# Transposing the attention weights of differential attention by DMA alone, with a third pair of score banks

## The chip, the cores and the metric

One Trainium2 chip, eight cores, each running the same program on its own batch element of a batch of eight. The time is the device time of the slowest core, in microseconds (us).

## The reference, cut to what matters

Per batch element: 2048 tokens, width 2048, 16 query heads and 4 key/value heads of size 128. Each head has two query and two key projections, and its attention weights are a second softmax over the difference of two softmaxes.

```python
xn = _layernorm(x)
q = _rope((xn @ Wq).reshape(b, s, 16, 256));  k = _rope((xn @ Wk).reshape(b, s, 4, 256))
energy = einsum('bqhad,bkhad->bahqk', qd, kd)          # a = 0, 1: two score maps
energy = where(causal, -1e30, energy)
scores = softmax(energy / sqrt(128), axis=-1)
diff = softmax(where(causal, -1e30, scores[:, 0] - lam * scores[:, 1]), axis=-1)
att  = einsum('bhqv,bvhd->bqhd', diff, v)
att  = att * rsqrt(mean(att * att, -1) + 1e-8) * rms_w * (1 - LAM_INIT)
s = att.reshape(b, s, E) @ Wo
g = silu(ffn(xn))      # Hadamard transform, 8-bit activations, ternary weights, squared relu, twice
return x + s * g
```

## The kernel before

The program is a row of stages, one after the other. The stage that matters here is the attention, from about 2795 to 6785 us of the profiled span. Before it lie the weight scales, the layer norm and the projections, after it the output projection and the two layers of the feed-forward part.

The attention loops over 16 heads, and in each head over four groups of queries (`qc` = 0 to 3, 512 queries each). A group has four query tiles of 128 rows (`qs` = 0 to 3; `qt` = 4 qc + qs is the tile's number in the sequence). For each query tile, in program order:

- **Scores.** For each chunk of up to 512 keys (`nch` = qc + 1 of them, the last one is the diagonal chunk), TensorE makes the two score maps into the PSUM banks `psE0[b]` and `psE1[b]` (L746, L750). VectorE adds the causal triangle to the last 128 columns of the diagonal chunk (`trif`, L762, L764). ScalarE takes the exponentials and their sums (L769, L772), which frees the bank pair. There are two pairs, used in turn.
- **Difference.** VectorE works out the two reciprocals (`rstep`, L781 to L786) and the difference (`dif`, L798 to L806), and ScalarE its exponential into `Pf` (`expP`, L811).
- **Normalize.** VectorE scales the row into the bfloat16 tile `Pb` (`pnorm`, L822 to L825).
- **Transpose.** The tile's weights, qt + 1 blocks of 128x128, are brought into `PT`, keys on partitions. Blocks of even number go by a DMA transpose each, issued by SyncE (`ptp_e`, L837). Blocks of odd number are transposed one by one on TensorE into one of two PSUM buffers `psT4` (L849), and copied to `PT` by VectorE (L862) or ScalarE (L867) in turn.

After the four tiles of a group: `zset` (L880) sets the six 128x128 blocks of `PT` that lie above the diagonal to zero on VectorE; `attmm` (L890) multiplies values by `PT`, 4 qc + 4 matmuls; then come the square (L900), its sum over partitions (L903), a copy (L907), a small store by SyncE (L910) and the scaled copy of the result (L915).

What orders the work is written out by hand. Each step names the engine and the earlier steps it waits for, and the class `Ch` turns this into semaphore waits. Every engine works through its own steps in program order, so a step that waits holds all later steps of that engine. SyncE, besides, waits after a step for the landing of its own transfer when a later step names it as the last of its lane; for `ptp_e` this holds for the fourth tile of a group alone. The step `zset` waits for "the step added just before it" (`after=[steps.__len__() - 1] + ...`), whatever step that is. `pnorm` and the transposes of a group wait for the `attmm` of the group before. The next head's queries are loaded by SyncE ahead of the head's first tile.

Of the kernel before, what the change touches and what calls it, by code (L numbers as in the profile page):

```python
# [8 lines left out]
F32 = mybir.dt.float32  # L9
BF16 = mybir.dt.bfloat16  # L10
# [4 lines left out]
T = 2048  # L15
# [140 lines left out]
def build_program(taps=(), upto=99):  # L156
    nc = bass.Bass("TRN2", target_bir_lowering=False)
# [28 lines left out]
    out = dt("out", [T, E], F32, "ExternalOutput")  # L186
# [13 lines left out]
    with st:  # L200
# [23 lines left out]
        idn_s = sbuf("idn_s", [128, 128], BF16)  # L224
# [6 lines left out]
        with ExitStack() as ph:  # L231
# [13 lines left out]
                          lambda e, inc, _l=loads: [inc(e.dma_start(out=d[:, :], in_=s[:, :]), 16)  # L245
                                                    for d, s in _l])]
# [22 lines left out]
        with ExitStack() as ph:  # L269
# [12 lines left out]
            for i, (w, r, c) in enumerate(tiles):  # L282
# [4 lines left out]
                                  lambda e, inc, _w=w, _r=r, _c=c, _i=i:  # L287
# [3 lines left out]
                                  after=[prev_red] if prev_red >= 0 else -1))  # L291
# [178 lines left out]
        with ExitStack() as ph:  # L470
# [24 lines left out]
            def add(stp):  # L495
                steps.append(stp)
                return len(steps) - 1
# [133 lines left out]
        with ExitStack() as ph:  # L631
# [25 lines left out]
            taub = sb("taub", [128, 512], F32)  # L657
            taurow = sb("taurow", [1, 2 * 512], F32)
            psE0 = [ph.enter_context(nc.psum_tensor(f"psE0{i}", [128, 512], F32)) for i in range(2)]
            psE1 = [ph4i.enter_context(nc.psum_tensor(f"psE1{i}", [128, 512], F32)) for i in range(2)]  # L660
            psAt = ph4i.enter_context(nc.psum_tensor("psAt", [128, 512], F32))
            psRo = ph4i.enter_context(nc.psum_tensor("psRo", [128, 512], F32))
            psT4 = [ph4i.enter_context(nc.psum_tensor(f"psT4{i}", [128, 128], BF16))
                    for i in range(2)]
            psRp = psRo

            qc_glob = [0]
# [1 line left out]
            tptb_ctr = [0]  # L669
            tp_evac_b = {0: -1, 1: -1}  # L670
            steps = []
            idx_exp_bank = {0: -1, 1: -1}
            idx_attmm_prev = -1
            idx_attts_prev = -1
            idx_sq_prev = -1
# [21 lines left out]
            for g in range(KVH):  # L697
                gp_ = g % 2
                for hl in range(4):
# [27 lines left out]
                    for qc in range(4):  # L727
# [5 lines left out]
                        for qs in range(4):  # L733
# [4 lines left out]
                            for kc in range(nch):  # L738
                                cw = 512 if kc < qt // 4 else (qt % 4 + 1) * 128
                                isdiag = (kc == qt // 4)  # L740
                                bank = pair_glob[0] % 2
                                pair_glob[0] += 1

                                def mme(e, inc, _qt=qt, _kc=kc, _cw=cw, _b=bank,
                                        _gp=gp_, _hp=hp_):
                                    e.matmul(psE0[_b][:, 0:_cw],  # L746
                                             qh[_hp][:, _qt * 128:(_qt + 1) * 128],
                                             kg[_gp][:, _kc * 512:_kc * 512 + _cw],
                                             start=True, stop=True)
                                    inc(e.matmul(psE1[_b][:, 0:_cw],  # L750
                                                 qh[_hp][:, T + _qt * 128: T + (_qt + 1) * 128],
                                                 kg[_gp][:, T + _kc * 512: T + _kc * 512 + _cw],
                                                 start=True, stop=True))
                                i_mm = add(Step("tensor", 1, mme,
                                                after=[i_qload, i_kvload,
                                                       idx_exp_bank[bank]]), tag="E")
                                kv_used[gp_].append(i_mm)
                                q_used[hp_].append(i_mm)
                                i_pre = i_mm
                                if isdiag:  # L760
                                    def trif(e, inc, _cw=cw, _b=bank):
                                        e.tensor_add(psE0[_b][:, _cw - 128:_cw],  # L762
                                                     psE0[_b][:, _cw - 128:_cw], tri_s[:, :])
                                        inc(e.tensor_add(psE1[_b][:, _cw - 128:_cw],  # L764
                                                         psE1[_b][:, _cw - 128:_cw], tri_s[:, :]))
                                    i_pre = add(Step("vector", 1, trif, after=[i_mm]), tag="E")

                                def expf(e, inc, _kc=kc, _cw=cw, _b=bank, _p=par):
                                    e.activation(e0b[:, _p * T + _kc * 512: _p * T + _kc * 512 + _cw],  # L769
                                                 psE0[_b][:, 0:_cw], AF.Exp, scale=ISQ,  # L770
                                                 accum_out=A0[:, _p * 4 + _kc:_p * 4 + _kc + 1])
                                    inc(e.activation(e1b[:, _p * T + _kc * 512: _p * T + _kc * 512 + _cw],  # L772
                                                     psE1[_b][:, 0:_cw], AF.Exp, scale=ISQ,
                                                     accum_out=A1[:, _p * 4 + _kc:_p * 4 + _kc + 1]))
                                i_exp = add(Step("scalar", 1, expf,
                                                             after=[i_pre, last_pn[par]]), tag="E")
                                idx_exp_bank[bank] = i_exp
                                idx_exp_last = i_exp
# [50 lines left out]
                                            after=[idx_expP_last, idx_attmm_prev]), tag="P")  # L829
                            last_pn[par] = i_pn  # L830

                            n_even = (qt + 2) // 2
                            n_odd = (qt + 1) // 2

                            def ptp_e(e, inc, _qt=qt, _qs=qs, _of=PTof):
                                for kt in range(0, _qt + 1, 2):
                                    inc(e.dma_start_transpose(  # L837
                                        PT[:, _of + kt * 512 + _qs * 128: _of + kt * 512 + (_qs + 1) * 128],
                                        Pb[:, _qs * T + kt * 128: _qs * T + (kt + 1) * 128]), 16)
# [1 line left out]
                                            after=[i_pn] + idx_ptp_prev[ptpar]), tag="T")  # L841
                            idx_ptp_cur.append(i_tp)
                            last_tp[par] = i_tp
                            for kt in range(1, qt + 1, 2):
                                tb = tptb_ctr[0] % 2
                                tptb_ctr[0] += 1
                                i_tt = add(Step("tensor", 1,
                                               lambda e, inc, _kt=kt, _qs=qs, _tb=tb:
                                               inc(e.transpose(psT4[_tb][:, :],  # L849
                                                               Pb[:, _qs * T + _kt * 128:  # L850
                                                                  _qs * T + (_kt + 1) * 128],
                                                               idn_s[:, :])),
                                               after=[i_pn, tp_evac_b[tb]] + idx_ptp_prev[ptpar]),
                                           tag="T")
                                ee = "scalar" if (tptb_ctr[0] % 2 == 0) else "vector"

                                def tevac(e, inc, _kt=kt, _qs=qs, _of=PTof, _tb=tb):
                                    inc(e.tensor_copy(
                                        PT[:, _of + _kt * 512 + _qs * 128:
                                           _of + _kt * 512 + (_qs + 1) * 128],  # L860
                                        psT4[_tb][:, :]) if False else
                                        e.tensor_copy(  # L862
                                        PT[:, _of + _kt * 512 + _qs * 128:
                                           _of + _kt * 512 + (_qs + 1) * 128],
                                        psT4[_tb][:, :]))
                                def tevac_s(e, inc, _kt=kt, _qs=qs, _of=PTof, _tb=tb):
                                    inc(e.copy(out=PT[:, _of + _kt * 512 + _qs * 128:  # L867
                                                      _of + _kt * 512 + (_qs + 1) * 128],
                                               in_=psT4[_tb][:, :]))
                                i_ev4 = add(Step(ee, 1, tevac_s if ee == "scalar" else tevac,  # L870
                                                 after=[i_tt]), tag="T")
                                tp_evac_b[tb] = i_ev4
                                idx_ptp_cur.append(i_ev4)
                        zblocks = [(kt, qs) for kt in range(4 * qc + 4) for qs in range(4)
                                   if 4 * qc + qs < kt]

# [526 lines left out]
```

How the kernel before makes its waits and increments, by code:

```python
                def body(eng, _e=ename):  # L125
                    for i, s in enumerate(steps):
                        if s.eng != _e:
                            continue
                        preds = _preds(i, s)
                        if preds:
                            tg = {}
                            for j in preds:
                                ln, c = post[j]
                                tg[ln] = max(tg.get(ln, 0), c)
                            for ln, c in tg.items():
                                eng.wait_ge(self.sems[ln], c)
                        else:
                            for ln, c in base.items():
                                if c > 0:
                                    eng.wait_ge(self.sems[ln], c)
                        mysem = self.sems[s._lane]
                        got = {"n": 0}
                        def inc(instr, k=1, _g=got, _s=mysem):
                            _g["n"] += k
                            return instr.then_inc(_s, k)
                        s.fn(eng, inc)
                        assert got["n"] == s.inc, \
                            f"step {i} ({s.eng}): declared inc {s.inc} != emitted {got['n']}"
                        if s.eng in ("sync", "gpsimd") and i in waited:
                            eng.wait_ge(mysem, post[i][1])
# [54 lines left out]
        def vsync(e, instr):  # L206
            instr.then_inc(vssem, 1)
            vs_n[0] += 1
            e.wait_ge(vssem, vs_n[0])
            return instr
```

## Time and profile before

| | us |
|---|---|
| median of 2 runs | 10589.99 |
| lowest and highest | 10569.17, 10610.82 |
| profiled execution | 10586.41 |
| its span on the slowest core (core 6) | 10584.8 |
| spans of the eight cores | 10537.4 to 10584.8 |

The profile is that of one execution on core 6. Its engines are PE (TensorE matmul), PEld (TensorE weight load), DVE (VectorE), ACT (ScalarE), POOL (GpSimd) and SP (SyncE). SPq stands for SyncE's sequencer, which issues DMAs and is not counted as a busy engine. The rows read from the trace stand in a section of their own below.

### The profile page before, as it was taken

The numbers are of one execution on the slowest core, as the hardware profiler recorded it, in microseconds if no ns is written. First come the engines' busy times: TensorE is split into PE (matmuls) and PEld (weight loads), VectorE is DVE, ScalarE is ACT, GpSimd is POOL, SyncE is SP. The second block draws the span as 40 slices with busy tenths as digits, with TensorE's granted clock in tenths as the row PEclk, the third lists the DMA queues.
The fourth block names the chain that finished last, engine by engine and source line by source line (L and its number), as shares of the span: only waits on it lengthen the run. The fifth ranks groups of instructions, "written<-read, shape, count | busy, mean of one in ns | idle before, by whom it ended". The sixth has DMA issues, their size and how long they took to land. (4 is left out here: it accounts for less than half of the span.)

```text
span 10584.8 us, 65816 instructions; the slowest of 8 cores (10537.4 to 10584.8 us)
## 1 busy us (share of the span) xinstructions
PE 3650.6 (34%) x12334; PEld 1337.9 (13%) x12334; DVE 3547.4 (34%) x9994; ACT 2182.6 (21%) x6008; POOL 961.7 (9%) x1684
## 2 busy tenths in 40 slices
PE   0010004555522222222222222355577201014777
PEld 0000002222200000000000000012233100001222
DVE  5114432222333333333333333210011465653221
ACT  0220002222333333333333333200122100000110
POOL 0000004444000000000000000013111000000111
PEclk9999999777655555555555555557788655556777
DMA  6210004333100000000000000012333101011222
GB/s 235 71 49 19 18 24 92 67 67 70 37 14 14 13 19 14 14 14 20 15 16 20 14 14 14 8 14 34 92 103 100 40 17 32 17 32 56 78 85 70
DMA packets 622508, 462.31 MB, mean 44 GB/s; under 512 B 366329, under 2 KB 572394, under 8 KB 611362
## 3 DMA queue, kind: packets, MB, share of 16 engines
q1 hardware_dynamic: 437538, 269.24, 9.2%
q0 software_dynamic: 184576, 188.85, 7.9%
q8 instruction: 120, 1.97, 0.1%
q14 instruction: 274, 2.24, 0.1%
HBM read 350.52 MB, written 98.57 MB: 42 GB/s over the span
## 5 line engine op out<-in xcount | busy, mean ns | idle before, releaser
L849 PE MATMUL psT<-idn_s,Pb 128*128 128x128 bf16 x1024 | 268.0, 265 | 2206.0 <-DVE Pb L825 2076.2
L1298 PE MATMUL psD<-K,tsl 128*128 128x512 bf16 x2048 | 613.9, 473 | 86.5 <-DVE tsl L1276 86.5
L1057 PE MATMUL psU<-xqs,tsl 128*128 128x512 bf16 x2048 | 522.8, 423 | 180.4 <-DVE tsl L1047 180.4
L980 POOL DMA_DIRECT2D wost<-wo x256 | 136.0, 592 | 4296.3 <-DVEq L123 4258.1
L811 ACT ACTIVATE Pf<-e0b 128x512 f32<-128x512 bf16 (+3 forms) x640 | 362.1, 566 | 781.0 <-DVE e0b L802 515.9
L602 PE MATMUL psP<-xns,wqst 128*128 128x512 bf16 x2048 | 487.1, 402 | 28.7 <-ACT Xs L612 26.2
L769 ACT ACTIVATE e0b<-psE 128x512 bf16<-128x512 f32 (+3 forms) x640 | 341.6, 534 | 422.4 <-DVE psE L764 264.5
L746 PE MATMUL psE<-kg,qh 128*128 128x512 bf16 (+3 forms) x640 | 327.9, 513 | 270.3 <-DMA qh<-qT_h 151.0
L849 PEld LDWEIGHTS psT<-idn_s,Pb 128*128 128x128 bf16 x1024 | 106.9, 104 | 2464.2 <-issue 2451.9
L616 DVE TENSOR_TENSOR m1b<-Xc,ctab 128x512 f32<-128x512 f32 x160 | 110.7, 692 | 858.0 <-ACT Xs L612 857.9
L890 PE MATMUL psAt<-PT,vg 128*128 128x512 bf16 x640 | 254.1, 574 | 370.3 <-DMA PT<-Pb 370.3
L762 DVE TENSOR_TENSOR psE<-psE,tri_s 128x128 f32<-128x128 f32 x256 | 76.6, 299 | 830.4 <-PE psE L750 830.4
L750 PE MATMUL psE<-kg,qh 128*128 128x512 bf16 (+3 forms) x640 | 343.6, 539 | 0.0
L990 PE MATMUL psE<-attT,wost 128*128 128x512 bf16 x1024 | 260.0, 421 | 234.1 <-DMA wost<-wo 234.1
L772 ACT ACTIVATE e1b<-psE 128x512 bf16<-128x512 f32 (+3 forms) x640 | 339.3, 530 | 0.0
L1102 DVE TENSOR_TENSOR W2f<-W2f 128x256 f32<-128x256 f32 x640 | 218.3, 419 | 335.8 <-ACT W2f L1161 332.5
L602 PE MATMUL psP<-xns,wkst 128*128 128x512 bf16 x512 | 126.8, 411 | 508.0 <-DMA wqst<-wq 507.4
L1298 PEld LDWEIGHTS psD<-K,tsl 128*128 128x128 bf16 x2048 | 233.9, 116 | 442.3 <-issue 306.9
L867 ACT COPY PT<-psT 128x128 bf16<-128x128 bf16 x512 | 136.2, 266 | 729.9 <-PE psT L849 729.9
L1191 PE MATMUL psR<-mrow,onr 1*128 1x256 f32 x16 | 9.5, 694 | 789.0 <-DVE betar L1186 789.0
L1057 PEld LDWEIGHTS psU<-xqs,tsl 128*128 128x128 bf16 x2048 | 216.2, 107 | 486.9 <-issue 297.2
L526 POOL DMA_DIRECT2D wqst<-wq x512 | 273.0, 975 | 13.0 <-issue 13.0
(180 smaller groups left out, 6670.3 us busy)
## 6 DMA issues: line engine op xcount, KB each, us to landing
xns<-xnT_h SPq DMA_DIRECT2D x256, 128.0 KB
wstg<-wupT SPq DMA_DIRECT2D x512, 64.0 KB
h_h<-h2b POOLq DMA_DIRECT2D x128, 256.0 KB, 2.5
W2f<-h_h SPq DMA_DIRECT2D x256, 128.0 KB
wst<-wdnT SPq DMA_DIRECT2D x512, 64.0 KB
PT<-Pb SPq DMA_TRANSPOSE x1152
wst<-wupT SPq DMA_DIRECT2D x16, 1024.0 KB
wst<-wupT POOLq DMA_DIRECT2D x16, 1024.0 KB, 5.5
```

Of the source, the lines that this page charges most:

```text
L526: inc(e.dma_start(out=wqst[_p][:, (hl * 2 + c2) * 2048 + ec * 128: (hl * 2 + c2) * 2048 + (ec + 1) * 128], in_=wq[ec * 128:(ec + 1) * 128, ...
L602: mm = e.matmul(psP[_b][:, :], _w[:, _wc + ec * 128: _wc + (ec + 1) * 128], xns[_xp][:, ec * 512:(ec + 1) * 512], start=(ec == 0), stop=(e ...
L746: e.matmul(psE0[_b][:, 0:_cw], qh[_hp][:, _qt * 128:(_qt + 1) * 128], kg[_gp][:, _kc * 512:_kc * 512 + _cw], start=True, stop=True)
L750: inc(e.matmul(psE1[_b][:, 0:_cw], qh[_hp][:, T + _qt * 128: T + (_qt + 1) * 128], kg[_gp][:, T + _kc * 512: T + _kc * 512 + _cw], start=T ...
L769: e.activation(e0b[:, _p * T + _kc * 512: _p * T + _kc * 512 + _cw], psE0[_b][:, 0:_cw], AF.Exp, scale=ISQ, accum_out=A0[:, _p * 4 + _kc:_ ...
L772: inc(e.activation(e1b[:, _p * T + _kc * 512: _p * T + _kc * 512 + _cw], psE1[_b][:, 0:_cw], AF.Exp, scale=ISQ, accum_out=A1[:, _p * 4 + _ ...
L811: inc(e.activation(Pf[:, _kc * 512: _kc * 512 + _cw], e0b[:, _p * T + _kc * 512: _p * T + _kc * 512 + _cw], AF.Exp, accum_out=Zc[:, _p * 4 ...
L849: inc(e.transpose(psT4[_tb][:, :], Pb[:, _qs * T + _kt * 128: _qs * T + (_kt + 1) * 128], idn_s[:, :])),
L890: mm = e.matmul(psAt[:, :], vg[_gp][:, kt * 128:(kt + 1) * 128], PT[:, _of + kt * 512: _of + (kt + 1) * 512], start=(kt == 0), stop=(kt == ...
L990: mm = e.matmul(psS[_b][:, :], wost[_p][:, ec * 128:(ec + 1) * 128], attT[:, ec * T + _tc * 512: ec * T + (_tc + 1) * 512], start=(ec == 0 ...
L1057: mm = e.matmul(psU[_b][:, :], tsl[_p][:, ec * 128:(ec + 1) * 128], xqs[:, ec * T + _tc * 512: ec * T + (_tc + 1) * 512], start=(ec == 0), ...
L1298: mm = e.matmul(psD[_b][:, :], tsl2[_p][:, ec * 128:(ec + 1) * 128], K2[:, ec * T + _tc * 512: ec * T + (_tc + 1) * 512], start=(ec == 0), ...
```

## The change

Three edits, all in the attention stage.

1. All blocks of a query tile go by DMA transpose: `ptp_e` loops over every block instead of every second one, and the loop over the odd blocks (the transposes on TensorE and their copies on VectorE and ScalarE) is gone. Over a head, SyncE issues 136 DMA transposes instead of 72, and 64 TensorE transposes with 64 copies go.
2. The two PSUM buffers `psT4` are gone, and a third pair of score banks `psE0[2]`, `psE1[2]` takes their place. Chunks use the three pairs in turn.
3. Nothing is edited in `zset`, but the step added just before it is now another one: `ptp_e` of the group's fourth tile, where it was the last copy out of `psT4`.

```diff
-            psE1 = [ph4i.enter_context(nc.psum_tensor(f"psE1{i}", [128, 512], F32)) for i in range(2)]
+            psE0.append(ph4i.enter_context(nc.psum_tensor("psE02", [128, 512], F32)))
+            psE1 = [ph4i.enter_context(nc.psum_tensor(f"psE1{i}", [128, 512], F32)) for i in range(3)]
...
-            psT4 = [ph4i.enter_context(nc.psum_tensor(f"psT4{i}", [128, 128], BF16))
-                    for i in range(2)]
...
-            idx_exp_bank = {0: -1, 1: -1}
+            idx_exp_bank = {0: -1, 1: -1, 2: -1}
...
-                                bank = pair_glob[0] % 2
+                                bank = pair_glob[0] % 3
...
-                            n_even = (qt + 2) // 2
-                            n_odd = (qt + 1) // 2
+                            n_even = qt + 1
+                            n_odd = 0
 
                             def ptp_e(e, inc, _qt=qt, _qs=qs, _of=PTof):
-                                for kt in range(0, _qt + 1, 2):
+                                for kt in range(0, _qt + 1, 1):
                                     inc(e.dma_start_transpose(
...
-                            for kt in range(1, qt + 1, 2):
-                                tb = tptb_ctr[0] % 2
-                                tptb_ctr[0] += 1
-                                i_tt = add(Step("tensor", 1,
...
-                                               inc(e.transpose(psT4[_tb][:, :],
...
-                                               after=[i_pn, tp_evac_b[tb]] + idx_ptp_prev[ptpar]),
-                                           tag="T")
-                                ee = "scalar" if (tptb_ctr[0] % 2 == 0) else "vector"
...
-                                i_ev4 = add(Step(ee, 1, tevac_s if ee == "scalar" else tevac,
-                                                 after=[i_tt]), tag="T")
-                                tp_evac_b[tb] = i_ev4
-                                idx_ptp_cur.append(i_ev4)
```

## Rows read from the trace of the kernel before

**Rows 1.** The page: the span in 40 slices, in tenths.

```profile
PE   0010004555522222222222222355577201014777
...
PEclk9999999777655555555555555557788655556777
```

**Rows 2.** Waits in the attention: who waited for whom, total us, times, longest.

```profile
PE psT L849 <- DVE Pb L825: 2076.2, 240, 11.3
...
PE psAt L890 <- DMA PT<-Pb: 370.3, 64, 9.1
...
DVE PT L880 <- ACT PT L867: 43.8, 64, 1.2
```

**Rows 3.** Waits of SP's own queue in the attention, same columns.

```profile
SPq L136 <- DVE Pb L825: 1761.6, 256, 10.2
```

**Rows 4.** Timeline of SP, first group, then last head: start, us, what, how many.

```profile
2801.67 22.70 SPq L837 DMA_TRANSPOSE PT<-Pb  x6
...
6549.32 23.21 SPq L837 DMA_TRANSPOSE PT<-Pb  x6
...
6587.30 35.94 SPq L837 DMA_TRANSPOSE PT<-Pb  x14
...
6640.30 50.10 SPq L837 DMA_TRANSPOSE PT<-Pb  x22
...
6711.52 62.79 SPq L837 DMA_TRANSPOSE PT<-Pb  x30
```

**Rows 5.** Timeline of SP, single stretches: bursts of 4 and 8, two slow issues.

```profile
6618.31 4.92 SPq L837 DMA_TRANSPOSE PT<-Pb  x4
...
6764.28 10.02 SPq L837 DMA_TRANSPOSE PT<-Pb  x8
...
2839.81 1.81 SPq L837 DMA_TRANSPOSE PT<-Pb  x1
...
6730.53 2.28 SPq L837 DMA_TRANSPOSE PT<-Pb  x1
```

**Rows 6.** Line 837: duration in ns, minimum, median, maximum, first and last start.

```profile
L837 SPq DMA_TRANSPOSE PT<-Pb x1152: 1094/1232/2555, 2801.7 to 6773.1; - x192
```

**Rows 7.** Timeline, last head, tiles 0 to 2: start, us, engine, line, operation.

```profile
6548.89 0.29 DVE L825 TENSOR_SCALAR Pb<-Pf,r 128x128 bf16<-128x128 f32 x1
6549.09 0.29 DVE L762 TENSOR_TENSOR psE<-psE,tri_s 128x128 f32<-128x128 f32 x1
...
6554.10 0.35 DVE L825 TENSOR_SCALAR Pb<-Pf,r 128x256 bf16<-128x256 f32 x1
...
6555.85 0.30 DVE L762 TENSOR_TENSOR psE<-psE,tri_s 128x128 f32<-128x128 f32 x1 [0.54 <-PE psE L750]
```

**Rows 8.** Timeline, last head, tile 4 to tile 5.

```profile
6586.61 0.55 DVE L825 TENSOR_SCALAR Pb<-Pf,r 128x640 bf16<-128x640 f32 x1
...
6589.18 0.60 ACT L769 ACTIVATE e0b<-psE 128x512 bf16<-128x512 f32 x1 [0.80 <-PE psE L750]
...
6590.33 0.38 ACT L769 ACTIVATE e0b<-psE 128x256 bf16<-128x256 f32 x1
...
6595.89 0.62 DVE L825 TENSOR_SCALAR Pb<-Pf,r 128x768 bf16<-128x768 f32 x1
```

**Rows 9.** Timeline, last head, end of the group of tiles 4 to 7.

```profile
6617.44 0.75 DVE L825 TENSOR_SCALAR Pb<-Pf,r 128x1024 bf16<-128x1024 f32 x1
6618.44 0.60 PE L849 MATMUL psT<-idn_s,Pb 128*128 128x128 bf16 x2 [8.17 <-DVE Pb L825]
...
6620.51 0.87 DVE L880 MEMSET PT<- 128x128 bf16 x6 [0.62 <-ACT PT L867]
6624.68 3.57 PE L890 MATMUL psAt<-PT,vg 128*128 128x512 bf16 x8 [4.76 <-DMA PT<-Pb]
```

**Rows 10.** Timeline of PE: the values' matmuls of the last two groups.

```profile
6691.89 5.09 PE L890 MATMUL psAt<-PT,vg 128*128 128x512 bf16 x12 [6.42 <-DMA PT<-Pb]
...
6775.75 5.00 PE L890 MATMUL psAt<-PT,vg 128*128 128x512 bf16 x16 [7.79 <-DMA PT<-Pb]
```

More of the change, by code:

```diff
@@ L843, in build_program @@
                             last_tp[par] = i_tp
-                            for kt in range(1, qt + 1, 2):
-                                tb = tptb_ctr[0] % 2
-                                tptb_ctr[0] += 1
-                                i_tt = add(Step("tensor", 1,
-                                               lambda e, inc, _kt=kt, _qs=qs, _tb=tb:
-                                               inc(e.transpose(psT4[_tb][:, :],
-                                                               Pb[:, _qs * T + _kt * 128:
-                                                                  _qs * T + (_kt + 1) * 128],
-                                                               idn_s[:, :])),
-                                               after=[i_pn, tp_evac_b[tb]] + idx_ptp_prev[ptpar]),
-                                           tag="T")
-                                ee = "scalar" if (tptb_ctr[0] % 2 == 0) else "vector"
[L857 to L869, printed above, removed]
-                                i_ev4 = add(Step(ee, 1, tevac_s if ee == "scalar" else tevac,
-                                                 after=[i_tt]), tag="T")
-                                tp_evac_b[tb] = i_ev4
-                                idx_ptp_cur.append(i_ev4)
                         zblocks = [(kt, qs) for kt in range(4 * qc + 4) for qs in range(4)
```

## The prediction, made before the changed kernel was timed

> **What bounds the kernel now.** The slices of the page [rows 1] come first. In the attention, slices 11 to 25, PE stands at 2 and 3 tenths and no engine is full. The stage is therefore a chain of waits and not a full engine, and its length is what it takes to go through that chain. The list of waits for this stretch shows the two links that the change touches [rows 2]. PE waits 2076.2 us for `pnorm` with a transpose at the head of its queue, 240 times: every score matmul of the next query tile stands behind these transposes. And 64 times, once in a group, PE waits for the landing of the DMA transposes before it can multiply by the values: 370.3 us. The third view is SP's own queue [rows 3]: it idles 1761.6 us for `pnorm`. That is SP's whole slack ahead of its transposes.
>
> The timeline of SP gives the length of each group [rows 4]: from the first issue of tile 0 to the end of the last issue of tile 3 it takes 23.21, 35.94, 50.10 and 62.79 us in the last head. Over all 64 such stretches (64 rows, the first 22.70, the last 62.79) the means are 23.2, 36.1, 50.7 and 63.2, together 173.3 us a head. What follows in a group (landing, the values' matmuls, square, sum, copy, the first tile of the next group) hardly depends on who transposed. So I compare this stretch before and after.
>
> **What one DMA transpose costs.** SP is held for the whole issue: the median record of line 837 lasts 1232 ns [rows 6]. A burst of four takes 4.92 us, one of eight 10.02 [rows 5], so each further one costs (10.02 - 4.92) / 4 = 1.275 us. Besides, 42 of the 1152 records, one in 27, last over 1.3 us; the first and last of them are 1.81 and 2.28 [rows 5], about 0.8 over the median, which adds 0.03 each. I take 1.305 us. The engines behind keep up: the values' matmuls start 6624.68 - (6618.31 + 4.92) = 1.45 us after the last issue of a burst of four, and 6775.75 - (6764.28 + 10.02) = 1.45 after one of eight [rows 5, 9, 10]. If transfers piled up, the longer burst would land later. So the price is the issue on SP, and it adds up.
>
> The Trainium skill ("VectorE: DVE Perf Modes", The three transpose paths) gives 390 ns for a 128x128 bf16 transpose on TensorE and 1309 ns by the DMA crossbar, and its rules say to use TensorE where PSUM will do. That rule speaks against this change, and the trace agrees with its DMA figure within 3%; with 1.309 in place of my 1.305 the sum would move by less than 10 us.
>
> **What the removal gives.** Without transposes in PE's queue, the scores of the next tile are done long before they are wanted, and ScalarE goes on to the first chunks while VectorE normalizes. Before, this happens only from tile 0 to tile 1, since tile 0 has no odd block: the triangle of tile 1 starts 0.20 us after the start of tile 0's scaling [rows 7]. From tile 1 to tile 2 it starts 6555.85 - 6554.10 = 1.75 after it; with the row above as the pattern (0.20, and 0.06 for the longer scaling) it would be 0.26. That saves 1.5 us. Tile 3 saves about 1.8, since its score matmuls and the scaling before it are wider (an estimate). In group 1 the exponentials of tile 5's diagonal chunk start at 6590.33 [rows 8]. After the change the first chunk's exponentials, 6590.33 - 6589.18 = 1.15 us, need not wait for the scaling that starts at 6586.61 (ScalarE is free by then), so they are over by 6587.7. The triangle follows the scaling by the same pattern: 0.46 after 6586.61, two additions of some 0.5 together and 0.1 of handover, 6587.7 as well. That saves 2.6 to 2.7 us, and about as much or a little more for tile 6. These times are the chain's. The question is whether SP keeps up.
>
> **Group by group,** first issue to end of last issue, after the change:
> - Group 0, 10 transposes: the chain rules. The 23.2 shrink by 1.5 + 1.8, and the last burst grows from two transposes to four, 2 x 1.275: 23.2 - 3.3 + 2.5 = 22.4.
> - Group 1, 26 transposes: tile 5's scaling starts 6595.89 - 6586.61 = 9.3 us after tile 4's [rows 8], 9.35 with the longer scaling, and after the change 6.65 (five transposes take 6.5, so SP just waits). From there the chain would take some 7.2 us to tile 6 (an estimate: 6.65 and about 0.5 for 128 more keys), but six transposes take 7.8: SP rules. 6.65 + 21 x 1.305 = 34.0.
> - Group 2, 42 transposes: SP is never free. 42 x 1.305 = 54.8.
> - Group 3, 58 transposes: 58 x 1.305 = 75.7.
>
> Together 187.0 (unrounded) against 173.3 us: **+13.7 us a head**. Groups 0 and 1 gain about 0.8 and 2.1, group 2 loses 4.1, group 3 loses 12.5. What the shorter chain gives in groups 2 and 3 is hidden behind SP.
>
> **The step nobody edited.** `zset` waits for the step before it. That was the last copy out of `psT4`: 43.8 us over 64 groups, and the six memsets were over 3.3 us ahead of the values' matmuls (6620.51 + 0.87 against 6624.68) [rows 2, 9]. Now that step is the fourth tile's `ptp_e`, so the memsets start when the transposes have landed, and the matmuls wait for them: 0.87 for the six [rows 9], and a handover from VectorE to PE, which takes 6618.44 - (6617.44 + 0.75) = 0.25 [rows 9]. 1.1 us x 4 groups = **+4.4 us a head**. At least it costs the 0.87 alone (3.5 a head).
>
> **At nothing** I cost three things. The 64 copies a head that leave VectorE and ScalarE are already in the savings above, or lie beside SP's longer burst. The third bank pair: with one chunk the next tile needs one pair, and with three or four the exponentials free a pair every 1.15 us, so that a second pair came back in time as well; its cover is the wait for SP, and were that gone it would be part of the faster rival below. The larger number of landings: 1.45 us after the last issue, as now. Unknown is the clock of the values' matmuls, which come after a longer idle time of PE. In the last head 12 of them take 5.09 us, 0.42 each, which is the 1.2 GHz level, and 16 take 5.00 [rows 10], partly at 2.4 GHz. Were all sixteen at the lower level it would be 6.8: at most +1.8 a head, +29 us, at least nothing. I take nothing into the sum and keep the 29 for the range.
>
> **The sum.** (13.7 + 4.4) x 16 heads = +290 us on the profiled execution's 10586.4, which is 3.6 under the median of the runs: 10876 us, taken as 10875, 2.7% slower. 2% of 10590 is 212 us, about what a measurement of this kernel can tell from no change.
>
> **The rivals.**
> - *Same mechanism, cheaper issues: within 2%.* By the groups above the loss a head is 121 x (price) - 139.9 us (121 transposes are in the terms where SP rules). The 2% line (13.2 a head) lies at 1.265 us each, and a burst of eight costs 10.02 / 8 = 1.25 [rows 5] when counted from a fresh start. With 1.25 it is 11.4 a head, +182 us, and with the memsets at 0.87 as well 10.5, +168: 10755. For it: the slow issues could fall where SP waits anyway. Against it: they come once in 27 transposes, busy or not, and three of four groups now have no wait left.
> - *Issues in a long burst run at the price of a lone one.* The shortest record is 1.094 [rows 6], 1.10 with the step to the next. Then groups 2 and 3 take 46.2 and 63.8, groups 0 and 1 about 21.9 and 30.5: 162.4 + 4.4 against 173.3, -6.5 a head, -104 us: 10480. Against it: the second to eighth of a burst never run so fast now.
> - *The transposes are as good as free: faster.* If SP only hands them over and the chain rules everywhere, each tile but a group's first saves what its diagonal exponentials gain: 3.3 a head in group 0, about 9.4 in group 1, and by the same reckoning some 16 in group 2 and 20 in group 3. 49 x 16 = 780 us, less 70 for the memsets: about 9875. It decides as soon as a transpose costs less than some 1.03 us of SP (6.7 more a head than in the rival above, over some 104 transposes). Against it stand the bursts of four and eight.
> - *Longer bursts meet a limit the bursts of eight don't show* (SP held by a full queue). Then each issue costs more; 10% on 1.305 gives 15.8 more a head, +253: 11130. Against it: no growth of the landing time from four to eight.
>
> For the free-transposes rival the Trainium skill has a rule too ("Advanced Engine Details and Errata", X-Bar Transpose): such a DMA is as fast as a regular one. The trace has SP held 1.232 us by each, whatever the transfer itself takes, so I give that reading little.
>
> **How the numbers follow.** My case, SP as the bound at 1.28 to 1.34 us with the memsets on the path: 0.66. Cheaper issues, within 2%: 0.22. Price of a lone issue: 0.04, also within 2%. Free transposes: 0.04. A queue limit: 0.04. So faster 0.04, within 2% 0.26, slower 0.70. The predicted time is 10875. The range runs from 10755 (1.25 each, memsets alone) to 10965 (1.33 each for +48, clock +29, and some slack); the last three cases lie outside.
>
> **What would show it.** SP's bursts in groups 2 and 3 should be one unbroken row, 42 and 58 transposes in about 55 and 76 us; the wait of SP for `pnorm` should fall from 1761.6 us to some 600, the first tile of each group and group 0. PE's wait of 2076.2 should vanish and reappear as a wait before the values' matmuls, over 1000 us in place of 370.3, released by the memsets of `zset` (or the landing). Group 0 and 1 should be slightly shorter than before. I am wrong if SP still waits for `pnorm` in group 3, if the spacing of issues isn't about 1.28, or if `attmm` starts ahead of the memsets.

## The result, and the profile after

| | before | after |
|---|---|---|
| median of the runs, us | 10630.1 (10 runs) | 10800.2 (11 runs) |
| profiled execution | 10586.4 | 10797.1 |
| its span, slowest core | 10584.8 (core 6) | 10795.5 (core 0) |

The ratio after to before is 1.0178, 95% interval [1.0151, 1.0204]: 1.8% slower. (The ratio is close to that of the runs' means, 10811.7 and 10623.1; the two medians alone would give 1.0160.) The median is inside the forecast range and 75 us under the predicted 10875.

First the page of the changed kernel, slices of the span in tenths, as in [rows 1].

```profile
PE   0010006555321111111111111155477311113776
...
PEclk9999998777655555555555555557688655556777
```

PE is emptier in the attention, 1 tenth instead of 2 and 3, and the stage is no shorter. Its granted clock still stands at 5 tenths, the 1.2 GHz level. Now the waits in the attention (who waited for whom, us in total, times, longest), first those of the engines, then those of SP's queue, which answer [rows 2, 3].

```profile
PE psAt L859 <- DVE PT L849: 2498.7, 64, 56.6
...
DVE PT L849 <- DMA PT<-Pb: 1463.7, 64, 44.3
```

```profile
SPq L136 <- DVE Pb L824: 634.7, 128, 10.4
```

PE's wait for `pnorm` (2076.2 us) is gone. In its place PE waits 2498.7 us before the values' matmuls, and what releases it is the memsets of `zset`. These in turn wait 1463.7 us for the landing of the transposes; before they waited 43.8 us for a copy. SP's own wait for `pnorm` fell from 1761.6 to 634.7 us: its slack is used up. The timeline of SP for the last head (start, us, what, how many) shows where, against the last four rows of [rows 4].

```profile
6749.90 22.64 SPq L836 DMA_TRANSPOSE PT<-Pb  x10
...
6787.67 33.35 SPq L836 DMA_TRANSPOSE PT<-Pb  x26
...
6840.31 54.12 SPq L836 DMA_TRANSPOSE PT<-Pb  x42
...
6916.27 73.84 SPq L836 DMA_TRANSPOSE PT<-Pb  x58
7000.58 0.51 SPq L879 DMA_DIRECT2D msb<-msrow  x1
```

The first two groups are shorter than before (23.21 and 35.94), the last two longer (50.10 and 62.79). The 58 transposes of group 3 take 73.84 / 58 = 1.273 us each without a pause. Over 16 heads the stretches' means are 22.6, 33.4, 53.6 and 74.2, together 183.7 us against 173.3.

Last, the end of the last group, which answers [rows 9, 10].

```profile
6988.88 1.23 SPq L836 DMA_TRANSPOSE PT<-Pb  x1
6991.44 0.87 DVE L849 MEMSET PT<- 128x128 bf16 x6 [42.39 <-DMA PT<-Pb]
6992.56 5.36 PE L859 MATMUL psAt<-PT,vg 128*128 128x512 bf16 x16 [54.78 <-DVE PT L849]
```

From the end of the last issue (6990.11) to the matmuls it is 2.45 us, where it was 1.45. Six memsets of 0.87 and a handover of 0.25 lie between.

**Where the 211 us of the two spans come from.** SP's store at the end of the attention is the row 7000.58 above; in the kernel before it is this one.

```profile
6783.40 0.51 SPq L910 DMA_DIRECT2D msb<-msrow  x1
```

From the first transpose to this store the attention took 6783.40 - 2801.67 = 3981.7 us before [rows 4]. After it took 7000.58 - 2794.74 = 4205.8 (2794.74 is the start of its first transpose): +224 us. Of these (183.7 - 173.3) x 16 = 166 lie in SP's stretches and 1.0 x 64 = 64 between last issue and matmuls; the rest (-6) is in the matmuls and first tiles. The stages around the attention, which have no edit, were 13 us faster in this execution than in that of the kernel before.

### The profile page after: what moved, and what is told of

The parts are those of the page before. It is cut to its first block and busy times, and to the rows that moved or that the text cites. A ratio compares the mean times of both kernels' runs of the same rounds, so it can differ in the third digit from the quotient of the medians.

```text
span 10795.5 us, 60187 instructions; the slowest of 8 cores (10727.6 to 10795.5 us)
## 1 busy us (share of the span) xinstructions
PE 3336.1 (31%) x11310; PEld 1216.9 (11%) x11310; DVE 3420.3 (32%) x9482; ACT 2015.3 (19%) x5496; POOL 962.0 (9%) x1684
## 3 DMA queue, kind: packets, MB, share of 16 engines
q1 hardware_dynamic: 601378, 302.93, 10.6%
## 5 line engine op out<-in xcount | busy, mean ns | idle before, releaser
L859 PE MATMUL psAt<-PT,vg 128*128 128x512 bf16 x640 | 250.2, 567 | 2498.7 <-DVE PT L849 2498.7
L745 PE MATMUL psE<-kg,qh 128*128 128x512 bf16 (+3 forms) x640 | 308.6, 486 | 865.5 <-ACT e1b L771 707.1
L849 DVE MEMSET PT<- 128x128 bf16 x384 | 55.6, 165 | 1464.0 <-DMA PT<-Pb 1463.7
L869 ACT ACTIVATE sqb<-psAt 128x512 f32<-128x512 f32 x64 | 38.2, 597 | 1894.6 <-PE psAt L859 1894.6
L859 PEld LDWEIGHTS psAt<-PT,vg 128*128 128x128 bf16 x640 | 79.6, 132 | 2682.0 <-issue 2671.7
L749 PE MATMUL psE<-kg,qh 128*128 128x512 bf16 (+3 forms) x640 | 321.6, 508 | 0.0
L801 DVE TENSOR_TENSOR e0b<-e0b,e1b 128x512 bf16<-128x512 bf16 (+3 forms) x640 | 246.6, 385 | 68.7 <-DVE e0b L799 2.7
L1130 ACT COPY W2f<-psH 128x256 f32<-128x256 f32 x128 | 47.7, 373 | 1104.8 <-PE psH L1124 1103.1
```

The lines of the kernel that those rows point to most:

```text
L745: e.matmul(psE0[_b][:, 0:_cw], qh[_hp][:, _qt * 128:(_qt + 1) * 128], kg[_gp][:, _kc * 512:_kc * 512 + _cw], start=True, stop=True)
L749: inc(e.matmul(psE1[_b][:, 0:_cw], qh[_hp][:, T + _qt * 128: T + (_qt + 1) * 128], kg[_gp][:, T + _kc * 512: T + _kc * 512 + _cw], start=T ...
L801: last = e.tensor_sub(e0b[:, sl], e0b[:, sl], e1b[:, sl])
L859: mm = e.matmul(psAt[:, :], vg[_gp][:, kt * 128:(kt + 1) * 128], PT[:, _of + kt * 512: _of + (kt + 1) * 512], start=(kt == 0), stop=(kt == ...
```

## The experiments

Each kernel was timed beside the kernel before on its own chip. The ratios are to that, and where two kernels ran on different chips the ratios are compared and not the times. My theory: SP is held about 1.27 us by each DMA transpose, 121 of them a head set the pace, and the memsets add 1 us to each group; the freed chain of the tiles is hidden behind SP.

**1. The zeroing off the path** (`a_zfree`).

```diff
-                                       after=[steps.__len__() - 1] + idx_ptp_prev[ptpar]), tag="Z")
+                                       after=[i_pn] + idx_ptp_prev[ptpar]), tag="Z")
```

> The changed kernel with one edit: the zeroing of the six blocks waits for the fourth tile's scaling, no longer for its DMA transposes. Theory (SP's issues set the pace, and the memsets stand on the path behind them): the step from the last issue to the values' matmuls falls from 2.46 us to 1.46, 64 times, so 64 us less than the changed kernel's 10797, about 10733; SP's stretches stay at 183.7 us a head. Rival (the memsets only moved and cost nothing, the loss is all SP's issues or the clock): no difference, 10797.

Measured: 10737 us, ratio 1.0140 [1.0093, 1.0187]. The intervals of this and of the changed kernel overlap, so the ratio alone doesn't settle it. The timeline does (last group, end of SP's burst and the matmuls):

```profile
6914.79 15.26 SPq L836 DMA_TRANSPOSE PT<-Pb  x12
6931.54 5.92 PE L859 MATMUL psAt<-PT,vg 128*128 128x512 bf16 x16 [53.80 <-DMA PT<-Pb]
```

6931.54 - 6930.05 = 1.49 us, and PE is now released by the landing. The stretches stay at 183.7 us a head. From the first transpose to the last store the attention takes 6940.11 - 2788.7 = 4151.4 us, 54 less than in the changed kernel; the values' matmuls, somewhat longer here (6.1 us against 5.5 in group 3, means of 16), take back the rest of the 64.

**2. The same wait added to the kernel before** (`b_zwait`), to see its price where SP doesn't rule.

```diff
-                                       after=[steps.__len__() - 1] + idx_ptp_prev[ptpar]), tag="Z")
+                                       after=[i_tp] + idx_ptp_prev[ptpar]), tag="Z")
```

> The kernel before with one edit: the zeroing waits for the fourth tile's DMA transposes, as it does by accident in the changed kernel. Theory (0.87 us and the handover fall on the path behind every landing): 64 times 1.0 us more than before, +64 us. Rival (0.25 us of handover were there already, the landing's own, and PE waits no longer for the memsets than for the landing): less than 20 us more.

Measured: 10633 us beside 10584, ratio 1.0055 [1.0038, 1.0072], which is +58 us (the medians differ by 48). In the traces the attention of core 0 grew by 61 us (3982.2 to 4043.0). The theory holds, and the rival's 20 us lie outside. So about a third of the change's loss is a wait that nobody wrote.

**3. Half of the issues** (`a_half`). Experiments 3 and 4 leave out a part of the transposed weights and set `PT` to zero once, ahead of the heads (a line that the diffs here leave out), so their output is not that of the kernel.

```diff
-                            n_even = qt + 1
+                            n_even = (qt + 2) // 2
-                                for kt in range(0, _qt + 1, 1):
+                                for kt in range(0, _qt + 1, 2):
```

> The changed kernel with the DMA transposes of the odd blocks left out (those blocks of the transposed weights stay zero), nothing put in their place; so the heads' weighted values are partial sums. SP issues 72 transposes a head instead of 136, and PE has none. Theory: SP is no longer the bound and the chain of the tiles is; by the prediction's reckoning a head takes 23.2 - 3.3, 36.1 - 9.4, 50.7 - 16 and 63.2 - 20, 124 us in place of 183.7, so about 950 us less than 10797: 9850. Rival (the removal of the TensorE transposes from PE's queue freed nothing, the chain is no shorter than before): the groups take 173 us a head as before, about 10630.

Measured: 9870 us, ratio 0.9303 [0.9247, 0.9360]. SP's last head:

```profile
5837.68 20.21 SPq L837 DMA_TRANSPOSE PT<-Pb  x6
...
5873.02 26.75 SPq L837 DMA_TRANSPOSE PT<-Pb  x14
...
5917.78 33.32 SPq L837 DMA_TRANSPOSE PT<-Pb  x22
...
5972.73 42.72 SPq L837 DMA_TRANSPOSE PT<-Pb  x30
```

With as many DMA transposes as the kernel before, and PE's queue free, a head takes 122.4 us (mean of 16) instead of 173.3. The expected 124 came from the same reckoning as the prediction's rival of free transposes. So the chain freed of the TensorE transposes and their copies is some 50 us a head shorter, of which SP's queue lets nothing through in groups 2 and 3. This run has the third bank pair too, and by experiment 7 some 3.6 of the 50 are the pair's.

**4. Half the data in as many issues** (`a_narrow`).

```diff
-                                        PT[:, _of + kt * 512 + _qs * 128: _of + kt * 512 + (_qs + 1) * 128],
-                                        Pb[:, _qs * T + kt * 128: _qs * T + (kt + 1) * 128]), 16)
+                                        PT[:, _of + kt * 512 + _qs * 128: _of + kt * 512 + _qs * 128 + 64],
+                                        Pb[0:64, _qs * T + kt * 128: _qs * T + (kt + 1) * 128]), 16)
```

> The changed kernel with each DMA transpose moving half the block: 64 of the 128 rows, as many issues (the other half of the transposed weights stays zero). Theory (the price is one issue on SP, whatever it moves): a spacing of 1.27 us and a time as that of the changed kernel, 10797. Rival (SP is held by the amount of rows or the transfer): a spacing of about 0.64 us, the chain of the tiles rules, and the time falls to about 9900.

```profile
6964.51 73.55 SPq L837 DMA_TRANSPOSE PT<-Pb  x58
```

That is the last group: 1.268 us each with 64 rows, 1.273 with 128. The time was 10846 us, ratio 1.0237 [1.0178, 1.0295]. The rival of a price by rows would have given about 9900. The 46 us over the changed kernel's time are not from the attention, whose stretches are 183.1 us a head; in the profiled execution the first transpose started at 2847.12 instead of 2794.74, so they came ahead of it. They go with the granted clock and not with the edit: in that execution cores 0 to 3 had a mean clock of 0.678 and 0.679 and began their transposes at 2837 to 2847 us, cores 4 to 7 had 0.686 and 0.687 and began at 2787 to 2804. The one execution in which all eight cores had 0.686 to 0.688 took 10796 us. What lowered the clock stays open.

**5. One issue for a whole query tile** (`a_wide`). Up to 16 blocks go by one DMA transpose, whose target is a three-dimensional view of `PT`.

```diff
-                                for kt in range(0, _qt + 1, 1):
-                                    inc(e.dma_start_transpose(
-                                        PT[:, _of + kt * 512 + _qs * 128: _of + kt * 512 + (_qs + 1) * 128],
-                                        Pb[:, _qs * T + kt * 128: _qs * T + (kt + 1) * 128]), 16)
-                            i_tp = add(Step("sync", 16 * n_even, ptp_e,
+                                inc(e.dma_start_transpose(
+                                    PT[:, _of: _of + (_qt + 1) * 512].rearrange(
+                                        "p (k c) -> p k c", c=512)[:, :, _qs * 128:(_qs + 1) * 128],
+                                    Pb[:, _qs * T: _qs * T + (_qt + 1) * 128]), 16)
+                            i_tp = add(Step("sync", 16, ptp_e,
```

> The changed kernel with one DMA transpose for all blocks of a query tile, up to 128x2048, so 16 issues a head instead of 136, the same work. Theory 1 (the price is one per instruction): SP is free, the chain of the tiles rules, and the last burst of a group is one issue; about 104 us a head in place of 183.7, 9520. Theory 2 (the price is one per 128x128 block, inside one instruction too): the same 183.7 us a head and 10797.

Measured: 9597 us, ratio 0.9064 [0.9021, 0.9106]. The line's row (duration in ns, minimum, median, maximum), then SP's last head, then the end of the last group:

```profile
L835 SPq DMA_TRANSPOSE PT<-Pb x256: 1140/1254/2166, 2783.4 to 5769.8; - x128
```

```profile
5608.86 18.91 SPq L835 DMA_TRANSPOSE PT<-Pb  x4
...
5642.97 22.82 SPq L835 DMA_TRANSPOSE PT<-Pb  x4
...
5685.75 27.44 SPq L835 DMA_TRANSPOSE PT<-Pb  x4
...
5736.88 34.90 SPq L835 DMA_TRANSPOSE PT<-Pb  x4
```

```profile
5769.77 2.01 SPq L835 DMA_TRANSPOSE PT<-Pb  x1
5774.26 0.87 DVE L849 MEMSET PT<- 128x128 bf16 x6 [4.62 <-DMA PT<-Pb]
5775.38 6.17 PE L859 MATMUL psAt<-PT,vg 128*128 128x512 bf16 x16 [17.00 <-DVE PT L849]
```

Theory 1 holds: the issue is priced by the instruction. Its records grow only from 1.15 us for one block to a mean of 1.84 for sixteen (16 records of each size), so a block in a wide issue costs SP about a tenth. SP's stretches take 103.7 us a head; 104 was expected. The time, though, is 77 us over the expected 9520, because landing after the last issue takes longer: 5774.26 - 5771.78 = 2.5 us to the memsets here instead of 1.3. Over all heads it is 2.5, 3.3, 3.6 and 3.8 us in the four groups from the end of the last issue to the values' matmuls, where one issue for each block had 2.45. That is about 55 us in all, a price of the wide issue that the expectation left out. The values' matmuls are longer as well, by about 16 us.

**6. Wide issues, zeroing off the path** (`a_wide_z`): experiments 1 and 5 together.

> One DMA transpose for each query tile (as in a_wide), and the zeroing waits for the fourth tile's scaling instead of its transposes. Theory (the memsets cost their own 0.87 us and the handover on the path behind the landing, whatever sets the pace before it): 64 us less than a_wide, 9597 - 64 = 9533. Rival (with SP free they no longer count): as a_wide, 9597.

Measured: 9550 us, ratio 0.8996 [0.8958, 0.9034], the fastest kernel of this study. Against `a_wide` the ratio falls by 0.0068, 72 us (the medians differ by 47, but the two ran on different chips). The intervals overlap a little, so the size is only roughly that of the expected 64. In the traces the attention shrank by 79 to 92 us, core by core: about 1.1 us at each of the 64 landings, and values' matmuls that are shorter in this run (5.3 us against 6.1 in group 3, core 4 in both).

**7. Wide issues with two bank pairs** (`a_wide_two`).

```diff
-                                bank = pair_glob[0] % 3
+                                bank = pair_glob[0] % 2
```

> One DMA transpose for each query tile (as in a_wide), but the chunks go by two pairs of score banks in turn instead of three. Theory (the third pair only matters once SP is no longer the bound): in groups 2 and 3 the diagonal chunk's scores wait for the exponentials of two chunks before; matmuls of 0.85 us, the triangle and two handovers take some 0.5 us longer than the chunk's exponentials (1.15) that hide them, 8 tiles a head, about +64 us: 9660. Rival (banks come back in time): 9597, within 10 us.

Measured: 9690 us, ratio 0.9117 [0.9088, 0.9146]. By ratios that is 0.0053 or 56 us over `a_wide`, and 0.0121 or 128 us over `a_wide_z`, which ran on the same chip, so 64 without the zeroing's 64. The last two groups of SP's last head, to be held against the 27.44 and 34.90 of `a_wide`:

```profile
5726.38 29.23 SPq L835 DMA_TRANSPOSE PT<-Pb  x4
...
5779.35 36.70 SPq L835 DMA_TRANSPOSE PT<-Pb  x4
```

Over 16 heads the stretches of groups 2 and 3 grow from 27.5 and 34.5 us to 29.3 and 36.3, 0.6 for each of their three steps, in groups 0 and 1 by nothing. That is the place and about the size expected: 3.6 us x 16 is 58. The attention as a whole grew a little less, 47 to 54 us core by core.

**8. Two bank pairs in the changed kernel** (`a_two`), the same edit there.

> The changed kernel with two pairs of score banks in turn instead of three, nothing else. Theory (SP's issues rule groups 2 and 3, where the third pair would matter, so it buys nothing in the changed kernel): 10797, within 10 us. Rival (the pair's gain, 94 us in the kernels with one DMA transpose for each tile, holds here too): about 10890.

Measured: 10801 us, ratio 1.0206 [1.0189, 1.0223] against 1.0178 of the changed kernel. The medians differ by 1 us, the ratios by 0.0028 (30 us), within their intervals; the rival's 94 would have given 1.0267. That 94 was the difference of medians from two chips; by ratios the pair's worth in the wide kernels is 56 to 64 us, and for that the timeline of SP decides, groups 2 and 3 of the last head:

```profile
6879.23 53.96 SPq L836 DMA_TRANSPOSE PT<-Pb  x42
...
6954.82 73.81 SPq L836 DMA_TRANSPOSE PT<-Pb  x58
```

The changed kernel has 54.12 and 73.84 there. Over all heads it is 183.5 us a head against 183.7: with SP as the bound the third pair buys nothing.

**9. The kernel before in another order** (`b_pipe`). The loop over the odd blocks (transposes and copies) is unedited but moved: a tile's stand behind the next tile's scores and exponentials, those of a group's last tile at the group's end.

```diff
+                            flush_t(pend, PTof, idx_ptp_cur, idx_ptp_prev[ptpar])
+
                             def rstep(e, inc, _n=nch, _h=h, _p=par):
...
+                            pend.append((i_pn, qt, qs))
+                        flush_t(pend, PTof, idx_ptp_cur, idx_ptp_prev[ptpar])
```

> The kernel before with one change of order: the TensorE transposes of a tile and their copies stand behind the next tile's scores and exponentials in the queues, instead of ahead of them. Half of the blocks by DMA, two bank pairs, all as before. Theory (before, PE waited 2076 us for the scaling with the next scores behind it, and that is what the change freed): near the chain's time as measured without odd transposes (9870), less 64 us for memsets off the path, plus some 60 for two bank pairs and 1 us a tile in three groups for the copies in VectorE's queue: about 10000. Rival (the order in PE's queue isn't what held the tiles): about 10590, as before.

Measured: 9992 us, ratio 0.9412 [0.9375, 0.9448]. PE's wait with a transpose at the head of its queue, to be held against [rows 2], and the last two groups of SP:

```profile
PE psT L705 <- DVE Pb L862: 855.2, 144, 8.6
```

```profile
6016.83 37.01 SPq L874 DMA_TRANSPOSE PT<-Pb  x22
...
6075.12 49.37 SPq L874 DMA_TRANSPOSE PT<-Pb  x30
```

The order alone brings most of what the change wanted (a ratio of 0.9412, where the chain without odd transposes and with a third bank pair had 0.9303), and it needs not one DMA transpose more than before.

**10. The same order, all on TensorE** (`b_allpe`).

```diff
-                    for kt in range(1, qt + 1, 2):
+                    for kt in range(0, qt + 1, 1):
```

(and `ptp_e` is gone).

> As b_pipe, but all blocks on TensorE and none by DMA: 136 transposes of 128x128 and 136 copies a head. Theory: SP is out of it, but a tile of group 3 needs 13 to 16 transposes at 0.43 us, 6 to 7 us of PE behind the scores, and the next tile's sums on VectorE stand behind the last copies: some 3 to 4 us more a tile than b_pipe in groups 2 and 3, and 3 us less at the end of a group, so about 10200. Rival (TensorE transposes are hidden once the order is right, as their 390 ns against 1.23 us of SP suggest): no more than b_pipe.

Measured: 10239 us, ratio 0.9650 [0.9609, 0.9692]. It is 247 us over `b_pipe` on the same chip. The rival falls: 136 transposes and copies a head don't hide, though each is short. The list of waits in the attention points at the place: ahead of the copies VectorE and ScalarE now wait 754.5 and 686.2 us for the transposes on PE, where `b_pipe` had 316.3 and 342.2. Each block has a copy of its own here, out of two buffers; several blocks in one bank with one wide copy were not tried, so this is the price of this form and not of TensorE transposes at large.

```profile
DVE PT L718 <- PE psT L705: 754.5, 992, 2.2
ACT PT L723 <- PE psT L705: 686.2, 912, 3.3
```

## Why the prediction was right, point by point

- **The mechanism.** Groups 0 and 1 shorter, groups 2 and 3 unbroken rows on SP, PE's wait moved to the values' matmuls and released by the memsets (2498.7 us, of which only "over 1000" was forecast), SP's wait for `pnorm` at "some 600" (634.7): all as put. Experiments 3, 4 and 5 exclude the other readings: with fewer issues or one for many blocks the time falls by 900 to 1200 us, with less data in as many issues it doesn't.
- **The chain.** Tile 5 was to be ready 6.65 us after tile 4. The changed kernel's timeline, first the scaling of tile 4 with the triangle behind it, then the scaling of tile 5:

```profile
6786.98 0.55 DVE L824 TENSOR_SCALAR Pb<-Pf,r 128x640 bf16<-128x640 f32 x1
6787.45 0.29 DVE L761 TENSOR_TENSOR psE<-psE,tri_s 128x128 f32<-128x128 f32 x1
...
6793.59 0.62 DVE L824 TENSOR_SCALAR Pb<-Pf,r 128x768 bf16<-128x768 f32 x1
```

  6793.59 - 6786.98 = 6.61 us, with 0.07 for the longer scaling 6.68; the triangle follows 0.47 after the scaling's start (0.46 forecast).
- **The mis-sized term: the slow issues.** The groups were forecast at 22.4, 34.0, 54.8 and 75.7 us and measured at 22.6, 33.4, 53.6 and 74.2. I took 1.305 us an issue, 1.275 and 0.03 for one slow record in 27, "busy or not". The 1.275 was right on this core (58 transposes in 73.9 us, mean of the heads' unbroken bursts, 1.275). The slow records nearly went: 11 over 1.3 us among 2176, where there were 42 among 1152. 121 x 0.03 x 16 = 58 us too much. With 1.275 the formula of the prediction gives 121 x 1.275 - 139.9 = 14.4 a head, +230 us, and the attention of the profile grew by 224.
- **The other cores, a test that nobody planned.** Cores of odd number issue faster in every run with one block to an issue. Here the median is 1.202 us instead of 1.232, and the spacing 1.244 instead of 1.275. Here is the changed kernel's line 836 on core 1, and its last group there, to be held against 73.84:

```profile
L836 SPq DMA_TRANSPOSE PT<-Pb x2176: 1077/1202/2001, 2789.8 to 6930.9; - x198
...
6859.84 72.28 SPq L836 DMA_TRANSPOSE PT<-Pb  x58
```

  In the kernel before that hardly counts: 172.7 us a head on odd cores, 173.2 or 173.3 on even ones. With SP as the bound it does: 180.1 to 180.2 against 183.6 to 183.7. At 1.244 the formula gives 10.6 a head, +170 us, and from the first transpose to the last store the odd cores grew by 177 on average, the even ones by 224. So the price of an issue sets the loss on either kind of core, and the time, which is that of the slowest core, goes by the even ones (10779 to 10796 us in the profiled execution, the odd ones 10728 to 10746). Why odd cores issue faster stays open.
- **The memsets.** 1.1 us a group was forecast, 1.0 measured: the handover from VectorE to PE takes 0.25, but the landing's own handover to PE, which it replaces, had a part of that. 6 us in all.
- **Cost at nothing.** The third bank pair is worth nothing here (experiment 8), with SP's queue as its cover, and it was worth about 60 us once the cover was gone (experiment 7). There I had argued that a second pair would come back in time as well; that was wrong, in a sentence that the sum didn't use. The matmuls' clock: sixteen took 5.36 us in the last group after, 5.00 before [rows 10], against a bound of 6.8; over all heads they are not slower (5.6 us against 5.9 in group 3, means of 16).
- **The chances.** 70% for slower by over 2%, 26% for within 2%. The runs give 1.8%, with 2% at the edge of the interval: the class that got the smaller chance. It is the one of the rival "same mechanism, cheaper issues", but that rival's own condition didn't come about where the time is set: its line lay at 1.265 us and the even cores have 1.275, for which the formula gives 2.2%. What brought it under 2% stood in no sum: the 10 runs of the kernel before have a median of 10630.1, not the 10590 that I started from, and the stages around the attention were 13 us faster in the profiled execution. That part is luck.

## What to carry to other kernels

Cost a DMA transpose by what it holds on its issuing queue, times the number of instructions, and compare that with the queue's slack group by group; if it doesn't fit, make one instruction carry many blocks before taking blocks to another engine. A step that waits for "the last one added" changes its meaning when that one is edited: look at what it waits for after each change. And where an engine in program order waits with independent work behind the waiting instruction, moving that instruction back can bring most of the gain of removing it.

## What the runs showed of the hardware

- **A DMA transpose holds SP for a nearly fixed time.** On cores of even number it is 1.23 us median for 128x128 (1.20 on odd ones), the same for 64 rows (73.55 us for 58), 1.25 median and 2.17 at most for 128x128 up to 128x2048. The Trainium skill ("VectorE: DVE Perf Modes", The three transpose paths) has 1309 ns for a 128x128 block by the crossbar. For a lone block the trace is near it (the median record is 6% shorter, the spacing of 1.275 us 3%), but as a price of the instruction and not of the block. The Trainium skill's rule on the same page (Rules for kernel authors), to take TensorE where PSUM will do, holds against one issue for each block: 10239 us with TensorE alone, 10800 with DMA alone. For wide issues it comes out the other way round. On one chip and with two bank pairs each, experiment 7 took 9690 us with DMA alone and experiment 10 took 10239 with TensorE alone and one copy for each block.
- **Slow issues go with fetches on an instruction queue.** This is the view of DMAs around the first slow issue of the kernel before, 2839.8 to 2841.6 us (queue, kind: packets, MB, share):

```profile
q1 hardware_dynamic: 281, 0.06, 18.5%
q8 instruction: 1, 0.02, 3.8%
```

  Before, on core 6, 40 of the 42 slow records have a record of queue 8 within 3 us of their start, and queue 8 has just 40 in the stretch from the first to the last transpose. After, it has 22, six of them within 3 us of a slow issue. PE's instructions in the attention, its sequencer's among them, fell in the same proportion (10235 to 5614, so that one record of queue 8 comes to 256 and to 255 of them), while VectorE's hardly fell (10271 to 9244) and ScalarE's neither (6858 to 5832). So queue 8 is probably PE's; before, PE reached new instructions at the very moment in which SP began its burst, since both waited for the same `pnorm`. The number of issues isn't what counts: with the same 1152 DMA transposes, core 0 has 42 slow records in the kernel before, 30 in `b_pipe` and 4 in `a_half`, which has no transposes in PE's queue. That fits, but it is read from the records; no run was made to test the cause, and it stays open.
